# Graph layer kernel: ScalarE copies the edges of all units up to 107 into one PSUM bank, not of the even ones alone

## Chip, cores and metric

One core of a Trainium2 chip. The metric is the device time of one execution in microseconds (us), lower is better.

## What is computed

Two graph layers over 6,250 nodes of 96 features and 106,250 edges sorted by their target node. Cut to what matters (the first layer's call passes `edge_attr_96` as `bases`; `x_feat` is the node table):

```python
h = _gelu(x_feat @ W_pre + b_pre)
msg = h[src] * bases                                  # the product
aggr = jax.ops.segment_sum(msg, dst, num_segments=n)
x = x_feat + aggr
y = _gelu(_gelu(x @ W1 + b1) @ W2 + b2)
return x + y
...
# second layer: the same edges, scaled by 1/sqrt of the degrees
h = x @ W_lin.T + b_lin
agg = jax.ops.segment_sum(h[src] * norm[:, None], dst, num_segments=n)
out = relu(agg + x @ W_root.T + b_root)
# each layer: x = layernorm(x + layer(x))
```

## The kernel before

The edges are cut into tiles of 128, five tiles make a **unit**: 166 units of 640 edges and a tail. What a unit needs:

- **Gather** (GpSimd, L923): five indirect DMAs, one a tile, bring the rows `h[src]` of the unit into the ring `gath`, which has GS = 8 slots. The gather of unit u waits until the product of unit u - 8 is done (`s_msg`). Units 0 to 4 are gathered otherwise, so L923 begins with unit 5.
- **Edges** (SyncE, L741): one DMA brings the edge features into the ring `edg`, ES = 4 slots.
- **One-hots** (VectorE, `hot`, L1352): a matrix per tile that says to which of 64 or 128 target nodes each edge belongs.
- **Product** (VectorE, `multiply`, L1376): `msg` = gathered rows x edges, ring of MS = 5. It reads `gath` in SBUF and, as its other operand, either `edg` in SBUF or the PSUM bank `edges_ps`.
- **Copy** (ScalarE, `copy_edges`, L1086): brings a unit's edges from `edg` into `edges_ps`, one bank for all. `by_bank(u)` (L129) says which units take this way: even ones below AHEAD = 108.
- **Sums** (PE, L1590): five matmuls into `seg` or `seg_odd`, by the parity of the group of units. Groups are three units up to unit 65 and one from unit 66 on, and there even units go to `seg`, odd ones to `seg_odd`. VectorE adds them to `sumT` (L1396).

Beside this, for the second layer, the kernel counts edges between blocks of source nodes and small windows of target nodes. **Pairs** of windows do it: VectorE **builds** the hots of four pairs (L1472 and L1474, two buffers), PE multiplies them (L1622, into `bank_q` and `bank_b` by turns), ScalarE **converts** the counts (`keep_pair`, L1026; where a store ends within a pair, L1029 and L1030). Units 3 to 104 have one or two builds each, so four or eight pairs. The counts go to HBM and come back as **pieces** (`piece_raw`, eight slots) with which PE does the second layer's sums (L1646, 12 matmuls a piece at first) and VectorE adds them (`dense`, L1499). Pieces use `bank_q` and the other bank of that kind; once no more edges are copied, `edges_ps` is their third bank (`last_copied`, `two_banks`). The node steps between the layers (`step0`) run on PE, ScalarE and VectorE in small phases in between.

Nothing is scheduled at run time. `schedule()` makes one list, `order`, and every engine walks it and issues its own part in this order, each waiting on semaphores. For unit u the list has the unit (hot and product on VectorE, sums on PE), the adds, the builds, and then at least eight slots with a pair, a node phase or a piece each. The copy of unit u + 1 stands in slot 2 of unit u:

```python
            if i == 2 and u < UNITS and by_bank(u + 1):
                order.append(("edges", u + 1))
```

So on ScalarE it stands behind the conversions of the first two pairs of unit u and ahead of the others. On PE, `hold` is a small weight load that waits for a semaphore (L1538).

Of the kernel before, what the change touches and what calls it, by code (L numbers as in the profile page):

```python
# [63 lines left out]
AHEAD = 108  # L64
# [63 lines left out]

def by_bank(u):  # L129

    return u % 2 == 0 and u < AHEAD


def reach(g):
# [193 lines left out]
def build(nc, x, xT_in, src, dst, first, tile_first, tile_rows, edge, edge_tail, W_pre, b_pre, W1, b1, W2, b2,  # L328
          WlinT, b_lin, WrootT, b_root, out):
    with ExitStack() as ctx:  # L330
# [3 lines left out]
        def sem(name):  # L334
            return ctx.enter_context(nc.semaphore(name))
# [172 lines left out]
        s_msg = sem("s_msg")  # L508
        s_eps = sem("s_eps")
# [67 lines left out]
        def rooted_before(item):  # L577
# [6 lines left out]
            x[2] == r and order.index(("piece", q)) < last_pair for q, x in enumerate(pieces)))  # L584

        last_copied = max(u for u in range(UNITS) if by_bank(u))
        two_banks = sum(1 for r in range(len(runs)) if any(
            x[2] == r and order.index(("piece", q)) < sums_at(last_copied + 1) for q, x in enumerate(pieces)))
# [64 lines left out]
        def by_tile(bank, tiles, d=D):  # L653
            return bank[:, 0:tiles * d].rearrange("p (t d) -> p t d", d=d)
# [37 lines left out]
        def gathers_before(u):  # L692

            return sum(16 * len(sizes(v)) for v in range(EARLY, u + 1) if v % GS == u % GS)

        def edges_landed(u):
            return sum(16 * (1 if v < UNITS else len(TAILS)) for v in range(u + 1) if v % ES == u % ES)
# [14 lines left out]
        def slot_tiles(u):  # L712

            s = u % GS
            return slice(s * UT, s * UT + len(sizes(u)))
# [269 lines left out]
        def _(act):  # L985
# [92 lines left out]

            def copy_edges(u):
                if u > 0:  # L1080
                    act.wait_ge(s_msg, u - 1)
                else:
                    act.wait_ge(s_kb, 3)
                act.wait_ge(s_edge[u % ES], edges_landed(u))
                if u < UNITS:
                    act.copy(edges_ps[:, 0:UT * D], edg[:, u % ES].rearrange("p j d -> p (j d)")).then_inc(s_eps, 1)  # L1086
                else:
                    for j, k in enumerate(TAILS):
                        last = act.copy(edges_ps[0:k, j * D:(j + 1) * D], edg[0:k, u % ES, j, :])
                    last.then_inc(s_eps, 1)  # L1090

            act.wait_ge(s_w, 8 * 16)
            for item in order:
                what = item[0]
                if what == "edges":
                    copy_edges(item[1])
                elif what == "meta":
                    keep_windows()
                elif what == "pair":
                    keep_pair(item[1])  # L1100
                elif what == "step0":
                    step_0(item[1], item[2], item[2])
                elif what == "step1":
                    step_1(item[1], item[2], item[2])
# [175 lines left out]
        def _(dve):  # L1280
# [82 lines left out]
            def multiply(u):  # L1363
                s = u % MS
                if by_bank(u):
                    dve.wait_ge(s_eps, u // 2 + 1)
                    edges = by_tile(edges_ps, UT)
                else:
                    dve.wait_ge(s_edge[u % ES], edges_landed(u))
                    edges = edg[:, u % ES]  # L1370
                if u < EARLY:
                    dve.wait_ge(s_h, CHUNKS - (-(u + 1) * UT // CT))
                else:
                    dve.wait_ge(s_gath[u % GS], gathers_before(u))
                if u < UNITS:
                    dve.tensor_tensor(  # L1376
                        msg[:, s, :, 0:D], gath[:, slot_tiles(u), :], edges, ALU.mult).then_inc(s_msg, 1)
                else:
                    for j, k in enumerate(TAILS):
                        last = dve.tensor_tensor(msg[0:k, s, j, 0:D], gath[0:k, u % GS * UT + j, :],  # L1380
                                                 edges[0:k, j, :], ALU.mult)
                    last.then_inc(s_msg, 1)
# [118 lines left out]
            for item in order:  # L1501
                what = item[0]
                if what in ("unit", "hot"):
                    hot(item[1])
                if what in ("unit", "product"):
                    multiply(item[1])
                elif what == "add":
                    add(item[1])
                elif what == "meta":
                    merge_windows()  # L1510
                elif what == "flag":
                    judge()
                elif what == "build":
                    build_hots(item[1])
                elif what == "dense":
                    dense(item[1])
                elif what == "step0":
                    node_stage_0(dve, item[1], item[2], item[2])
                elif what == "step1":
                    node_stage_1(dve, item[1], item[2], item[2])  # L1520
# [306 lines left out]
```

## Time and profile before

| | |
|---|---|
| time, median of 3 runs | 1125.99 us (1120.19 to 1127.88) |
| the profiled execution | 1126.56 us |
| its span, first to last instruction | 1124.8 us |
| mean granted TensorE clock in it | 0.906 |
| indirect gathers L923 | 806 |
| products with edges in SBUF / in PSUM | 112 / 54 |

The profile is one execution. A span is the time of one instruction or transfer from start to end; "idle before" is the time for which an engine stood still just before an instruction, with what ended it. "issue" means that the profile shows nothing it waited for. Times in the rows count from the start of the span. PEld is PE's weight load, which overlaps its matmuls. The clock is a share of TensorE's full 2.4 GHz.

### The profile page before, as it was taken

What the parts mean: (1) busy time and instruction counts of PE and PEld (TensorE: products, weight loads), DVE (VectorE), ACT (ScalarE), POOL (GpSimd) and SP (SyncE); (2) the same over time, 40 slices, a digit from 0 to 9 for tenths busy, and PEclk for the clock granted to TensorE, in tenths of its full rate; (3) what the DMA queues carried; (4) which work ended last, traced back from release to release, by engine and by line L of the source; (5) the groups of instructions that cost most, each with busy time, mean ns of one, the idle gap of its engine ahead of it and who ended that gap; (6) DMA issues with size and microseconds to landing.
All of it is one profiled execution on the core that took longest, in us unless ns stands there. A gap on an engine that the chain in (4) does not pass through costs nothing. (4 is left out here: it accounts for less than half of the span.)

```text
span 1124.8 us, 21017 instructions
## 1 busy us (share of the span) xinstructions
PE 938.3 (83%) x7410; PEld 792.9 (70%) x7847; DVE 719.1 (64%) x1521; ACT 473.2 (42%) x884; POOL 833.6 (74%) x917
## 2 busy tenths in 40 slices
PE   5877677677767887898889889899999989889786
PEld 5844445344444775685678678799999989789786
DVE  8976797677767667756576666634336454646567
ACT  1366685665665566555565556600001010001115
POOL 7877777777777777777777777777777777777715
PEclk9997986888877999696699999999999999879898
DMA  9457776675666769777788889998999997767853
GB/s 286 111 156 251 243 227 218 225 231 173 236 212 194 241 217 300 229 239 240 251 259 262 269 292 300 282 286 251 266 269 293 266 257 217 217 167 203 206 127 90
DMA packets 185723, 260.28 MB, mean 231 GB/s; under 512 B 68651, under 2 KB 163883, under 8 KB 179019
## 3 DMA queue, kind: packets, MB, share of 16 engines
q1 hardware_dynamic: 158049, 215.51, 59.7%
q0 software_dynamic: 26992, 42.82, 16.1%
q8 instruction: 61, 1.00, 0.4%
q10 hardware_dynamic: 569, 0.53, 0.2%
q14 instruction: 52, 0.42, 0.1%
HBM read 173.15 MB, written 85.62 MB: 230 GB/s over the span
## 5 line engine op out<-in xcount | busy, mean ns | idle before, releaser
L923 POOL DMA_INDIRECT gath<-table_h,srcs x806 | 784.6, 973 | 245.6 <-issue 242.5
L1646 PE MATMUL bank_q<-piece_raw,early_late 128*96 128x250 bf16 x2805 | 339.1, 273 | 8.2 <-DVE sumT L1499 6.0
L1646 PEld LDWEIGHTS bank_q<-piece_raw,early_late 128*96 128x96 bf16 x2805 | 304.9, 124 | 2.1 <-issue 0.5
L1026 ACT CAST counts_raw<-bank_q 128x490 bf16<-128x490 f32 x300 | 185.2, 617 | 201.9 <-PE bank_q L1622 198.7
L1026 ACT CAST counts_raw<-bank_b 128x490 bf16<-128x490 f32 x300 | 186.2, 621 | 46.8 <-PE bank_b L1622 46.1
L1622 PE MATMUL bank_q<-hots_raw 128*128 128x245 bf16 x626 | 134.9, 300 | 80.2 <-ACT counts_raw L1026 55.1
L1474 DVE TENSOR_TENSOR hots_raw<-counters,kb 128x1960 bf16<-128x1960 bf16 (+1 forms) x157 | 182.5, 1163 | 0.0
L1622 PE MATMUL bank_b<-hots_raw 128*128 128x245 bf16 x624 | 134.9, 301 | 19.9 <-ACT counts_raw L1026 7.1
L1590 PE MATMUL seg<-onehot,msg 128*97 128x64 f32 (+1 forms) x830 | 111.2, 290 | 23.9 <-DVE msg L1376 23.6
L1590 PE MATMUL seg_odd<-onehot,msg 128*97 128x64 f32 (+1 forms) x832 | 108.8, 286 | 23.3 <-DVE msg L1376 22.6
L1590 PEld LDWEIGHTS seg<-onehot,msg 128*97 128x97 f32 x830 | 103.2, 193 | 33.6 <-DVE msg L1376 31.6
L1472 DVE TENSOR_TENSOR hots_raw<-counters,kb 128x1024 bf16<-128x1024 bf16 (+1 forms) x157 | 106.8, 681 | 24.8 <-PE bank_b L1622 24.8
L1590 PEld LDWEIGHTS seg_odd<-onehot,msg 128*97 128x97 f32 x832 | 101.3, 189 | 29.8 <-DVE msg L1376 27.3
L1622 PEld LDWEIGHTS bank_q<-hots_raw 128*128 128x128 bf16 x626 | 44.6, 102 | 110.2 <-ACT counts_raw L1026 99.5
L1038 ACT ACTIVATE y<-bank_a,b1c 96x512 f32<-96x512 f32 (+2 forms) x14 | 8.8, 629 | 236.3 <-PE bank_a L1661 236.2
L1376 DVE TENSOR_TENSOR msg<-gath,edg 128x480 f32<-128x480 f32 x112 | 72.8, 650 | 48.6 <-DMA gath<-table_h,srcs 48.6
L1622 PEld LDWEIGHTS bank_b<-hots_raw 128*128 128x128 bf16 x624 | 50.1, 103 | 75.7 <-ACT counts_raw L1026 68.0
L1352 DVE TENSOR_TENSOR onehot<-counters,rel 128x320 f32<-128x320 f32 (+1 forms) x166 | 102.0, 614 | 0.0
L1376 DVE TENSOR_TENSOR msg<-gath,edges_ps 128x480 f32<-128x480 f32 x54 | 35.2, 652 | 81.1 <-ACT edges_ps L1086 81.0
L1499 DVE TENSOR_TENSOR sumT<-sumT,bank_q 96x250 f32<-96x250 f32 x91 | 37.1, 409 | 70.2 <-PE bank_q L1646 66.3
L1538 PEld LDWEIGHTS <-w_pre 97*128 97x128 bf16 x437 | 45.1, 109 | 51.8 <-DVE hots_raw L1474 27.0
L1646 PE MATMUL edges_ps<-piece_raw,early_late 128*96 128x250 bf16 x648 | 79.5, 273 | 0.0
(237 smaller groups left out, 796.7 us busy)
## 6 DMA issues: line engine op xcount, KB each, us to landing
counts_hbm<-counts_raw SPq DMA_DIRECT2D x50, 1531.2 KB
piece_raw<-counts_hbm SPq DMA_DIRECT2D x250, 250.0 KB
edg<-in_edge SPq DMA_DIRECT2D x166, 240.0 KB
gath<-table_h,srcs POOLq DMA_INDIRECT x806
piece_raw<-counts_hbm SPq DMA_DIRECT2D x38, 125.0 KB
piece_raw<-counts_hbm SPq DMA_DIRECT2D x25, 187.5 KB
counts_raw<-counts_hbm SPq DMA_DIRECT2D x4, 625.0 KB, 6.5
table_h<-stage SPq DMA_DIRECT2D x12, 192.0 KB, 5.4
```

The lines of the kernel that those rows point to most:

```text
L923: pool.indirect_dma_start(gath[0:k, u % GS * UT + j, :], None, table[0], bass.IndirectOffsetOnAxis(ap=srcs[0:k, t:t + 1], axis=0)).then_in ...
L1026: act.copy(counts[:, k % 2, :, i * WD:(i + 2) * WD].rearrange("p a (w n) -> p a w n", w=2), counted).then_inc(s_kept, 1)
L1038: act.activation(y1[0:D, 0:tiles * P], bank_a[0:D, 0:tiles * P], ACT.Gelu, bias=b1c[:, 0:1]).then_inc(s_y1, 1)
L1352: dve.tensor_tensor(onehot[:, s, :, 0:w], iota_ps[:, 0:w].unsqueeze(1).to_broadcast([P, UT, w]), rel[:, u * UT:(u + 1) * UT].unsqueeze(2). ...
L1376: dve.tensor_tensor(msg[:, s, :, 0:D], gath[:, slot_tiles(u), :], edges, ALU.mult).then_inc(s_msg, 1)
L1472: dve.tensor_tensor(hot_b(j)[:, 0:n], iota_b.unsqueeze(1).to_broadcast([P, n, P, 2]), blocks.unsqueeze(2).to_broadcast([P, n, P, 2]), ALU. ...
L1474: dve.tensor_tensor(hot_k(j)[:, 0:n], iota_k.unsqueeze(1).to_broadcast([P, n, KC, 2]), keys.unsqueeze(2).to_broadcast([P, n, KC, 2]), ALU. ...
L1499: dve.tensor_tensor(total, total, run_sum, ALU.add).then_inc(s_dense, 1)
L1538: pe.ldweights(w_pre[:].bitcast(BF16)[:, 0:P])
L1590: last = pe.matmul(group_sum(g), msg[0:k, u % MS, j, :], onehot[0:k, u % MS, j, 0:reach(g)], start=(u == first_unit(g) and j == 0), stop=( ...
L1622: last = pe.matmul(pair_bank(m)[:, w * KC:(w + 1) * KC], hot_b(j)[:, i, :, w], hot_k(j)[:, i, :, w], start=True, stop=True)
L1646: mm = pe.matmul(sums(r)[0:D, 0:DN], parts[:, FINE[c] + i, part, :], rows, start=(first and i == 0 and part == 0), stop=(last and i == til ...
```

## The change

`by_bank` now holds for every unit below 108. The 54 odd units below 108 get a copy, too, and their product reads `edges_ps`. As there is one bank, copy u must wait for product u - 1 (before: for u - 2, the product that had the bank last), and a product counts the copies by units.

```diff
 def by_bank(u):
 
-    return u % 2 == 0 and u < AHEAD
+    return u < AHEAD
...
             def copy_edges(u):
                 if u > 0:
-                    act.wait_ge(s_msg, u - 1)
+                    act.wait_ge(s_msg, u)
                 else:
                     act.wait_ge(s_kb, 3)
...
             def multiply(u):
                 s = u % MS
                 if by_bank(u):
-                    dve.wait_ge(s_eps, u // 2 + 1)
+                    dve.wait_ge(s_eps, u + 1)
                     edges = by_tile(edges_ps, UT)
```

ScalarE's queue of the kernel before, from the conversions of unit 77 over those of unit 78 to the copy of unit 80 (`s_edge0`: the slot of the ring `edg`):

```order
L1026 CAST counts_raw<-bank_b 128x49x10 [waits s_pair]
L1026 CAST counts_raw<-bank_q 128x49x10 [waits s_pair]
L1026 CAST counts_raw<-bank_b 128x49x10 [waits s_pair]
L1026 CAST counts_raw<-bank_q 128x49x10 [waits s_pair]
L1026 CAST counts_raw<-bank_b 128x49x10 [waits s_pair]
L1026 CAST counts_raw<-bank_q 128x49x10 [waits s_pair]
L1026 CAST counts_raw<-bank_b 128x49x10 [waits s_pair]
L1086 COPY edges_ps<-edg 128x480 [waits s_edge0,s_msg]
L1026 CAST counts_raw<-bank_q 128x49x10 [waits s_pair]
```

The same place of ScalarE's queue in the changed kernel:

```order
L1026 CAST counts_raw<-bank_b 128x49x10 [waits s_pair]
L1026 CAST counts_raw<-bank_q 128x49x10 [waits s_pair]
L1026 CAST counts_raw<-bank_b 128x49x10 [waits s_pair]
L1086 COPY edges_ps<-edg 128x480 [waits s_edge3,s_msg]
L1026 CAST counts_raw<-bank_q 128x49x10 [waits s_pair]
L1026 CAST counts_raw<-bank_b 128x49x10 [waits s_pair]
L1026 CAST counts_raw<-bank_q 128x49x10 [waits s_pair]
L1026 CAST counts_raw<-bank_b 128x49x10 [waits s_pair]
L1086 COPY edges_ps<-edg 128x480 [waits s_edge0,s_msg]
L1026 CAST counts_raw<-bank_q 128x49x10 [waits s_pair]
```

A copy for unit 79 has come in behind the first two conversions of unit 78, with the other conversions behind it. The rest of the queue is as it was.

VectorE's queue at unit 79, as a piece of the difference (the product of unit 79, ahead of it the add of a group's sum and the unit's one-hot, behind it the first build of the unit):

```order
 L1396 TENSOR_TENSOR sumT<-sumT,seg_odd 97x64
 L1352 TENSOR_TENSOR onehot<-counters,rel 128x5x64 [waits s_seg]
-L1376 TENSOR_TENSOR msg<-gath,edg 128x5x96 [waits s_gath7,s_edge3]
+L1376 TENSOR_TENSOR msg<-gath,edges_ps 128x5x96 [waits s_gath7,s_eps]
 L1472 TENSOR_TENSOR hots_raw<-counters,kb 128x1024 [waits s_pair]
 L1474 TENSOR_TENSOR hots_raw<-counters,kb 128x1960
```

Nothing changes its place. The product waits for ScalarE's copy (`s_eps`) in place of the edges' transfer (`s_edge3`). The queues of SyncE and GpSimd are the same in both kernels. PE has the same matmuls; from the first run of pieces in `edges_ps` on, the three banks of the runs come in another turn.

## Rows read from the trace of the kernel before

**Rows 1.** Groups by form: count | busy us, mean ns | idle before, what ended it.
```profile
L923 POOL DMA_INDIRECT gath<-table_h,srcs x806 | 784.6, 973 | 245.6 <-issue 242.5 <-DVE msg L1376 3.1
...
L1376 DVE TENSOR_TENSOR msg<-gath,edg 128x480 f32<-128x480 f32 x112 | 72.8, 650 | 48.6 <-DMA gath<-table_h,srcs 48.6
...
L1376 DVE TENSOR_TENSOR msg<-gath,edges_ps 128x480 f32<-128x480 f32 x54 | 35.2, 652 | 81.1 <-ACT edges_ps L1086 81.0
L1086 ACT COPY edges_ps<-edg 128x480 f32<-128x480 f32 x54 | 31.9, 591 | 0.7 <-DVE msg L1376 0.7
```
**Rows 2.** Windows: PE, PEld, DVE, ACT, POOL busy us; clock, DMA, GB/s.
```profile
170.00:383.00 213.00, 151.24 (x861) 99.44 (x923) 152.78 (x243) 129.70 (x242) 161.97 (x168) 0.82 0.66 213
383.00:735.00 352.00, 305.17 (x2422) 254.37 (x2540) 227.81 (x432) 205.16 (x369) 267.57 (x278) 0.91 0.83 261
735.00:968.00 233.00, 229.64 (x2147) 224.72 (x2238) 106.00 (x292) 13.89 (x21) 177.80 (x182) 0.99 0.91 266
968.00:1047.00 79.00, 66.69 (x538) 62.04 (x571) 42.27 (x128) 8.66 (x14) 60.10 (x63) 0.84 0.70 184
```
**Rows 3.** Timeline, gathers and products: start us, us, engine.
```profile
61.25 1.41 POOL L923 DMA_INDIRECT gath<-table_h,srcs  x1 [0.30 <-issue]
...
150.87 0.65 DVE L1376 TENSOR_TENSOR msg<-gath,edg 128x480 f32<-128x480 f32 x1
150.91 1.43 POOL L923 DMA_INDIRECT gath<-table_h,srcs  x1 [0.30 <-issue]
...
158.78 0.65 DVE L1376 TENSOR_TENSOR msg<-gath,edges_ps 128x480 f32<-128x480 f32 x1
158.90 0.94 POOL L923 DMA_INDIRECT gath<-table_h,srcs  x1 [0.30 <-issue]
...
161.39 0.94 POOL L923 DMA_INDIRECT gath<-table_h,srcs  x1 [0.31 <-issue]
161.76 0.65 DVE L1376 TENSOR_TENSOR msg<-gath,edg 128x480 f32<-128x480 f32 x1
...
740.39 1.40 POOL L923 DMA_INDIRECT gath<-table_h,srcs  x1 [0.31 <-issue]
```
**Rows 4.** The line L1376 in 170 to 383 us: what its engine waited for.
```profile
  DMA gath<-table_h,srcs: 32.4, 9
```
**Rows 5.** The same in 383 to 735 us; and who waited for it.
```profile
  ACT edges_ps L1086: 40.1, 18
...
  PEld seg L1590: 6.0, 7
...
  PEld seg_odd L1590: 2.1, 2
```
**Rows 6.** Timeline around unit 79.
```profile
538.66 0.65 DVE L1376 TENSOR_TENSOR msg<-gath,edg 128x480 f32<-128x480 f32 x1
...
539.82 1.17 DVE L1474 TENSOR_TENSOR hots_raw<-counters,kb 128x1960 bf16<-128x1960 bf16 x1
...
543.30 0.61 ACT L1026 CAST counts_raw<-bank_b 128x490 bf16<-128x490 f32 x1
...
545.93 0.62 PE L1622 MATMUL bank_q<-hots_raw 128*128 128x245 bf16 x2
```
**Rows 7.** L923 up to 726.6 us (min/median/max ns, first and last start); timeline there.
```profile
L923 POOL DMA_INDIRECT gath<-table_h,srcs x535: 940/944/1922, 44.8 to 725.4; - x179
...
722.60 0.66 DVE L1376 TENSOR_TENSOR msg<-gath,edges_ps 128x480 f32<-128x480 f32 x1 [0.94 <-ACT edges_ps L1086]
...
726.65 0.94 POOL L923 DMA_INDIRECT gath<-table_h,srcs  x1 [0.30 <-DVE msg L1376]
```
**Rows 8.** The line L1376 in 968 to 1047 us: what its engine waited for.
```profile
  DMA gath<-table_h,srcs: 16.2, 8
```
**Rows 9.** Windows of two stretches of 383 to 735 us.
```profile
441.00:568.00 127.00, 110.58 (x746) 85.80 (x783) 78.35 (x146) 69.72 (x127) 96.55 (x100) 0.77 0.76 240
568.00:735.00 167.00, 146.80 (x1305) 129.78 (x1363) 107.25 (x212) 98.28 (x175) 127.08 (x132) 1.00 0.89 277
```

## Prediction

> **What bounds the kernel now.** I read the groups first, for the engine whose work reaches from end to end. It is GpSimd with its 806 gathers [rows 1]: 784.6 us busy and 242.5 us idle "until issue". These add to 1027 us, and the idle time is the fixed 0.30 us that stands before every gather in the timeline [rows 3]. So GpSimd issues gathers from 44.8 us to about 1074 us with no pause, almost the whole span of 1124.8 us. A gather's median is 944 ns [rows 7] and its mean 973, which leaves 806 x 0.029 = 23 us of stretched gathers.
>
> Next I read the windows by stage [rows 2] and the product's waits [rows 4, 5]. They show who paces whom.
> - 170 to 383 us (units 23 to 56): VectorE waits 32.4 us for gathers before nine products, so the gathers pace.
> - 383 to 735 us (units 57 to 106): no product waits for a gather. PE is busy 305.2 of 352 us, and the products wait only for ScalarE's copies (40.1 us, 18 times). VectorE falls behind the gathers.
> - 735 to 968 us: PE is busy 229.6 of 233 us. What is late at 735 is late at 968.
> - 968 to 1047 us: products wait for gathers again (16.2 us, 8 times) [rows 8]; then comes the end.
>
> How far VectorE falls behind is in [rows 7]: 535 gathers have begun before 726.6, five a unit from unit 5 on, so the one at 726.65 is unit 112's first. It reuses the slot of unit 104, whose product ends at 722.60 + 0.66 = 723.26. GpSimd is 3.4 us from having to wait.
>
> **Removed: VectorE's second SBUF operand in 54 odd products.** A product takes 650 ns from SBUF and 652 ns from PSUM [rows 1], so VectorE itself gains nothing. GpSimd does. In [rows 3] an SBUF product starts at 150.87, the gather at 150.91 takes 1.43 us, 0.49 over the median; at 161.76 one starts inside a running gather, which stays at 0.94; at 158.78 a PSUM product is running when a gather starts, 0.94 again. So only a gather that starts while an SBUF product runs is stretched, to about the product's end. I laid all odd products up to unit 107 beside the gathers: 27 gathers over 1.00 us overlap one, from 61.25 (1.41) to 740.39 (1.40), the first and last in [rows 3], together 9.0 us over the median. 4.1 us lie before 383 us, 4.9 after. In one of them another SBUF operation shares the blame.
>
> The Trainium skill (GPSIMD Engine Reference, Key points) says that GpSimd shares its SBUF interfaces with VectorE, with contention for VectorE instructions with two SBUF inputs. Priced on every product's full length that would be 54 x 0.65 = 35 us, an estimate; the trace narrows it to gathers that begin under a product, 9 us, and the trace decides.
>
> **Added: 54 copies on ScalarE.** 54 x 0.591 = 31.9 us [rows 1]. ScalarE is busy 129.7 of 213 and 205.2 of 352 us in the two middle stages [rows 2], so as plain work they fit. Each stands behind the first two conversions of the unit ahead, and the later conversions stand behind it, so PE gets its bank back up to 0.6 us later.
>
> **The semaphore on the product before.** It adds nothing where hots are built (units 3 to 104): the two conversions ahead of copy u+1 need hots that VectorE builds after product u, so the queue imposes this order already. In units 1 and 3, by hand, the copy would end within 0.02 us of where the product starts now.
>
> **Moved: odd products wait for ScalarE.** This is the real cost. Behind a waiting product on VectorE stand the builds of the hots, and PE's pair products wait for these. Unit 79 [rows 6]: its product runs at 538.66 now, its first build ends at 540.99, 2.33 us after the product's start. The second conversion ahead of copy 79 (the one at 543.30) ends at 543.91; then copy 0.59, product at 544.53, build ready at 546.86. PE begins unit 79's first pair at 545.93, behind the unit's sums: that pair comes 0.9 us later. So a hold of 5.9 us costs PE 0.9, the rest lies under PE's own queue. Done for each of the 24 odd units from 57 to 103, eight holds are between 3.6 and 5.9 us, the others under 2.2 or none. I price six units like unit 79 (5.6 us; in the others PE arrives later than the hots) and 1.4 us for the added copies between conversions: 7 us of new PE waiting in this stage.
>
> The bounds are far apart. From below, even units already run this way: PE's weight loads wait 6.0 us for even products (seg) and 2.1 for odd ones (seg_odd) [rows 5]; doubling the difference adds 3.9 us. From above, all of VectorE's 40.1 us wait happens again and reaches PE: 40 us. I take 7, near the lower row, because that stage's PE idle time, 47 us, is mostly not caused by products.
>
> In 170 to 383 us the same holds come to 18 us (six odd units from 23 to 51), against 32.4 us of waiting for gathers. The gathers keep the pace with 14 us to spare, so this stage takes GpSimd's gain: -4.1 us at unit 57, at worst +4.
>
> **Other edits.** The first use of the copy bank by a piece moves from after unit 106 to after 107 and the banks of later runs rotate; the same matmuls remain. Nothing.
>
> **The sum.** At 735 us products stand at -4.1 + 7 = +2.9 us. GpSimd would be 8.5 us ahead by unit 112 (9.0 less the last stretch), but has only 3.4 us of room: the slot of unit 104 comes free at 723.3 + 2.9 = 726.2, so GpSimd now really waits, about 8 us, and leaves at -0.5 us. From there PE runs full to 968 (+2.9), the gathers run at -0.5. In 968 to 1047 PE idles 12 us and products wait 16.2 us for gathers: a PE chain late by 2.9 us catches up there, down to the gathers' -0.5. The end lies between -0.5 and +2.9; I take +1. The profiled execution took 1126.56 us, its span 1124.8; it lies 0.6 us above the median of 1125.99. 1126.56 + 1 = 1127.6, or 1127.0 beside the median. I say 1127.5. Here 9 us taken from the longest chain buy nothing, since they are used up by a ring of 8 units that has no room.
>
> **Rivals.**
> - **The ScalarE loop paces every unit (slower).** Place: products of odd units in 170 to 735 us. For: 40.1 us of such waits exist in even units alone [rows 5]. It decides once the gathers no longer pace by unit 57: then -4.1 becomes up to +4, and node steps on VectorE, which it now does ahead, show in odd units too; 0.9 us in 16 of the 24 units is 14 us. +4 + 14 = +18, less 2 absorbed behind 968: 1143. Against: 124 us of VectorE's 352 are idle. Chance 0.2.
> - **The clock (slower).** PE's granted clock is 0.77 in 441 to 568 us, where it is busy 110.6 of 127, and 1.00 in 568 to 735, busy 146.8 of 167 [rows 9]. 0.77 is a mean over stretches at 1.2 and at 2.4 GHz. If new gaps bring 0.77 to the second stretch, it can deliver 129 of its 146.8 us of busy work: 18 us at most, half of it 9: 1136. The Trainium skill (TensorE: Matmul & The Clock Gate, Part 1) ties this clock to PE's recent activity; by it new gaps could cost a stretch at 1.2 GHz, and no row here shows how many it would be. Chance 0.12.
> - **The gain arrives whole.** If a queue of ScalarE that is ahead hides the holds, and the PE-bound stage starts 9 us earlier: 1126.56 - 9.0 = 1117.6. Against: 3.4 us of room, and 12 us of PE idle behind 968. Chance 0.12.
> - The forecast, 1121 to 1134, has 0.5; 0.06 is for what I have not seen.
>
> **Range and chances.** 1118 to 1143 leaves out less than 2 in 10. What a measurement of this kernel tells from no change is about 1%, 11.3 us. Faster by more than that needs more than the 9.0 us there is: 0.04. Slower by more (from 1137.3) is the first slower rival and a third of the second: 0.22. Within: 0.74.
>
> **What would show it.** Right: edges_ps products x108, of which over 35 wait for L1086, some 80 us in 383 to 735; gathers at a median of 944 ns with total busy near 776 us; GpSimd waiting some 8 us for products between 640 and 740 us, where it waits for none now; PE idle up by 7 in 383 to 735; lag gone by 980. Wrong: products of 170 to 383 that never wait for gathers (first rival), a clock below 1.00 in 568 to 735 (second), no GpSimd wait at all and 735 reached 5 us earlier (third).

## The result and the profile after

The changed kernel takes 1135.0 us, the median of nine runs (1130.4 to 1137.99), beside 1122.65 us for the kernel before in as many (1120.19 to 1127.88). The ratio is 1.0094, with a 95% interval of 1.0077 to 1.0111: slower by just under 1%, 12.35 us between the medians. I had forecast 1127.5 us, no change that can be told. That stood on a median of three runs, 1125.99 us; against either median my forecast is a change of some +1 us, and 12.35 us came. One run of those told below, of `r_h` at 2104.54 us, stands in no median and no ratio. The profiled execution took 1135.81 us with a span of 1134.0 us (before: 1126.56 and 1124.8), at a mean granted clock of 0.901 (0.906).

The groups by form of the changed kernel, beside [rows 1]:

```profile
L923 POOL DMA_INDIRECT gath<-table_h,srcs x806 | 779.5, 967 | 263.4 <-issue 238.5 <-DVE msg L1376 24.9
...
L1376 DVE TENSOR_TENSOR msg<-gath,edges_ps 128x480 f32<-128x480 f32 x108 | 70.3, 651 | 169.1 <-ACT edges_ps L1086 168.8
L1086 ACT COPY edges_ps<-edg 128x480 f32<-128x480 f32 x108 | 63.4, 587 | 7.7 <-DVE msg L1376 7.7
L1376 DVE TENSOR_TENSOR msg<-gath,edg 128x480 f32<-128x480 f32 x58 | 37.7, 650 | 12.9 <-DMA gath<-table_h,srcs 12.9
```

The first row holds most of the case. The gathers' own time fell from 784.6 to 779.5 us, as it was meant to, by 5.1 us. Their idle time rose from 245.6 to 263.4 us, by 17.8 us, because GpSimd now waits 24.9 us for products where it had waited 3.1. The balance is +12.7 us, and the last gather starts at 1086.45 us, 12.6 us later than before. These two executions differ by 9.25 us in time, since from the start of the last gather to the end of the span the one before took 50.9 us and this one 47.6. The profiled execution of before is 3.9 us over its median; that 12.6 lies so near the 12.35 us of the medians is chance. The second row is why: products wait 168.8 us for copies in place of 81.0.

The windows, beside [rows 2] and [rows 9]:

```profile
170.00:383.00 213.00, 158.83 (x866) 103.64 (x928) 157.09 (x254) 141.41 (x268) 161.37 (x170) 0.81 0.65 213
383.00:735.00 352.00, 301.47 (x2358) 249.62 (x2477) 225.51 (x422) 211.57 (x387) 253.78 (x267) 0.91 0.80 255
735.00:968.00 233.00, 227.73 (x2124) 221.73 (x2210) 105.24 (x291) 20.86 (x33) 177.59 (x180) 0.99 0.89 263
968.00:1047.00 79.00, 70.83 (x564) 66.44 (x598) 43.74 (x131) 8.67 (x14) 60.41 (x62) 0.83 0.69 193
...
441.00:568.00 127.00, 108.47 (x733) 83.14 (x771) 78.68 (x144) 72.10 (x134) 96.23 (x102) 0.78 0.77 244
568.00:735.00 167.00, 145.68 (x1254) 128.01 (x1313) 104.76 (x205) 99.74 (x181) 113.74 (x120) 0.98 0.83 264
```

In 383 to 735 us GpSimd is busy 253.8 us instead of 267.6, PE 301.5 instead of 305.2: both lost time there. The clock in 568 to 735 us is 0.98, where it was 1.00: the sign that I had written down for the clock rival. It is small, but it will count below.

The product's waits, first in 170 to 383 us, beside [rows 4]:

```profile
  ACT edges_ps L1086: 52.8, 20
```

and in 383 to 735 us, beside [rows 5]:

```profile
  ACT edges_ps L1086: 83.5, 37
...
  POOL gath L923: 20.3, 11
  PEld seg L1590: 7.1, 8
  PEld seg_odd L1590: 6.0, 7
```

In the first of the two, "DMA gath" is gone from the list: where nine products had waited 32.4 us for gathers, none does now. In the second, the line "POOL gath" stands among those that wait for the product: GpSimd, 11 times, 20.3 us. PE's waits for odd products (seg_odd) rose from 2.1 to 6.0 us, by the 3.9 us of my lower bound.

How far each stage moved is read from the start of one product in both timelines (unit 56 ends the first stage, 104 the PE-bound one) and from the gathers. I give the changed kernel twice: the first execution, and one of a second measurement that is told below (`after_again`).

| start, us against before | changed | changed, again |
|---|---|---|
| first gather of unit 56 | -4.0 | -5.4 |
| product 56 (383.0) | +3.4 | -1.5 |
| product 96 | +6.4 | +1.6 |
| product 104 (722.6) | +11.7 | +6.8 |
| first gather of unit 112 (726.6) | +9.0 | +4.1 |
| product 147 (970.8) | +11.3 | +6.4 |
| last gather (1073.9) | +12.6 | +7.2 |
| time of these executions (1126.56) | +9.3 | +3.8 |
| time, medians | +12.4 | +6.9 |

### The profile page after: what moved, and what is told of

The parts are those of the page before. It is cut to its first block and busy times, and to the rows that moved or that the text cites. A ratio compares the mean times of both kernels' runs of the same rounds, so it can differ in the third digit from the quotient of the medians.

```text
span 1134.0 us, 21125 instructions
## 1 busy us (share of the span) xinstructions
PE 945.3 (83%) x7410; PEld 796.3 (70%) x7847; DVE 719.5 (63%) x1521; ACT 496.7 (44%) x938; POOL 828.6 (73%) x917
## 5 line engine op out<-in xcount | busy, mean ns | idle before, releaser
L923 POOL DMA_INDIRECT gath<-table_h,srcs x806 | 779.5, 967 | 263.4 <-issue 238.5
L1474 DVE TENSOR_TENSOR hots_raw<-counters,kb 128x1960 bf16<-128x1960 bf16 (+1 forms) x157 | 182.4, 1162 | 0.0
L1376 DVE TENSOR_TENSOR msg<-gath,edges_ps 128x480 f32<-128x480 f32 x108 | 70.3, 651 | 169.1 <-ACT edges_ps L1086 168.8
L1590 PE MATMUL seg<-onehot,msg 128*97 128x64 f32 (+1 forms) x830 | 114.9, 296 | 19.4 <-DVE msg L1376 19.2
L1590 PEld LDWEIGHTS seg<-onehot,msg 128*97 128x97 f32 x830 | 106.0, 197 | 30.1 <-DVE msg L1376 28.1
L1646 PEld LDWEIGHTS edges_ps<-piece_raw,early_late 128*96 128x96 bf16 x666 | 70.3, 123 | 0.0
```

What stands on the lines that cost most here:

```text
L923: pool.indirect_dma_start(gath[0:k, u % GS * UT + j, :], None, table[0], bass.IndirectOffsetOnAxis(ap=srcs[0:k, t:t + 1], axis=0)).then_in ...
L1376: dve.tensor_tensor(msg[:, s, :, 0:D], gath[:, slot_tiles(u), :], edges, ALU.mult).then_inc(s_msg, 1)
L1474: dve.tensor_tensor(hot_k(j)[:, 0:n], iota_k.unsqueeze(1).to_broadcast([P, n, KC, 2]), keys.unsqueeze(2).to_broadcast([P, n, KC, 2]), ALU. ...
L1590: last = pe.matmul(group_sum(g), msg[0:k, u % MS, j, :], onehot[0:k, u % MS, j, 0:reach(g)], start=(u == first_unit(g) and j == 0), stop=( ...
L1646: mm = pe.matmul(sums(r)[0:D, 0:DN], parts[:, FINE[c] + i, part, :], rows, start=(first and i == 0 and part == 0), stop=(last and i == til ...
```

## The experiments

All stand beside runs of the kernel before on the same chip, and a ratio is that of the kernel to it. They came in four sets. The diffs are against the changed kernel unless another is named.

**First set: what the parts do alone.** The change has three parts: relief (odd products don't read a second operand from SBUF), the work of 54 copies, and the hold (an odd product waits for ScalarE's queue).

`r_only` is the relief alone: the kernel before, in which odd products read the bank as it stands (the diff is against the kernel before; the pieces' first use of the bank is also moved behind unit 107, as in the change).

```diff
-                if by_bank(u):
+                if u < AHEAD:
                     dve.wait_ge(s_eps, u // 2 + 1)
+                    dve.wait_ge(s_edge[u % ES], edges_landed(u))
                     edges = by_tile(edges_ps, UT)
```

> Odd products up to unit 107 read the PSUM bank as it stands (the edges of the unit before, so the sums of odd units are left wrong), without a copy and without a wait for one. This is the relief of GpSimd alone. Theory 'hold' (odd products that wait for ScalarE are the loss): nothing is held, so this is faster than before by what the gather-paced stage can use, about 4 us: ratio 0.996; the product of unit 56 about 4 us earlier than before, that of unit 165 about 4 earlier. Rival 'all of it carries': 9 us, 0.992. Rival 'the PSUM operand itself costs': slower than before.

Measured: 1118.29 us, ratio 0.9968 [0.9953, 0.9983]. So the relief is worth 0.32% here, about 3.6 us (by the interval 1.9 to 5.3) of the 9 that I had counted. Its row of gathers shows where the gain comes from:

```profile
L923 POOL DMA_INDIRECT gath<-table_h,srcs x806 | 777.0, 964 | 245.8 <-issue 242.5 <-DVE msg L1377 3.3
```

The gathers are 7.6 us shorter in all, and GpSimd waits no more than before.

`c_only` is the copies' work alone: odd copies take a constant and odd products don't wait for them.

```diff
+                if u > 0:
+                    act.wait_ge(s_eps, u)
+                if u % 2 == 1:
+                    act.copy(by_tile(edges_ps, UT), iota[:, 0:D].unsqueeze(1).to_broadcast([P, UT, D])
+                             ).then_inc(s_eps, 1)
+                    return
...
-                if by_bank(u):
+                if by_bank(u) and u % 2 == 0:
```

> ScalarE makes the 54 added copies at their places (of a constant of the same shape, into the same bank), but odd products read SBUF and wait for nothing, as before. This is the copies' work alone. Theory 'hold': within 2 us of before, ratio 1.000 to 1.002. Rival 'work' (the copies push conversions and so PE's banks): 54 x about 0.2 us or more, 1.008 and up; the product of unit 56 late by 5 us or more against before.

Measured: 1124.18 us, ratio 1.0007 [0.9993, 1.0022]. 31.6 us of copies (54 of 0.585 us) are hidden as work, and what they do to PE's banks is too small to be told here.

`h_only` is the hold alone, with a copy of one column (0.194 us) in the place of the full one; odd products wait for it and read `edg`.

```diff
+                if u % 2 == 1:
+                    act.copy(tiny[:, 0:1], iota[:, 0:1]).then_inc(s_eps, 1)
+                    return
...
-                else:
+                if not by_bank(u) or u % 2 == 1:
                     dve.wait_ge(s_edge[u % ES], edges_landed(u))
                     edges = edg[:, u % ES]
```

> Odd products wait for ScalarE at the same place of its queue as in the change, but what stands there is a copy of one column, and they read SBUF as before. This is the hold alone. Theory 'hold': slower than before by all of the change's loss and the relief that it lacks, 12 to 16 us, ratio 1.011 to 1.014, with the product of unit 56 late by 5 or more. Rival 'work': nearly as before, under 4 us, 1.003.

Measured: 1127.28 us, ratio 1.0036 [1.0021, 1.0050]. These are 4 us where the theory of the hold wanted 12 to 16: the hold behind a short copy is not the whole loss.

`r_h` is both: the same small copy, and odd products read the bank as it stands.

```diff
+                if u % 2 == 1:
+                    act.copy(tiny[:, 0:1], iota[:, 0:1]).then_inc(s_eps, 1)
+                    return
...
                     dve.wait_ge(s_eps, u + 1)
+                    dve.wait_ge(s_edge[u % ES], edges_landed(u))
```

> The hold with a copy of one column, and odd products read the bank as it stands (sums of odd units left wrong): relief and hold, without the copies' work. Theory 'hold': as the change less up to 3 us, ratio 1.007 to 1.010. Rival 'work': 0.996 to 0.999.

Measured: 1121.64 us, ratio 0.9996 [0.9980, 1.0012], where 1.007 to 1.010 was expected. Relief and hold cancel, and the relief is worth 0.40% under this short hold. But the three parts add up to 1.0011 (0.9968, 1.0007 and 1.0036), and the whole is 1.0094. Something in the whole is more than its parts: the full copy in front of a held product had been in none of these kernels.

**Second set: the copy's length under the hold, and its place.** `full_front` keeps everything of the change but the relief: odd products wait for the full copy and read `edg`.

```diff
                 if by_bank(u):
                     dve.wait_ge(s_eps, u + 1)
                     edges = by_tile(edges_ps, UT)
-                else:
+                if not by_bank(u) or u % 2 == 1:
                     dve.wait_ge(s_edge[u % ES], edges_landed(u))
                     edges = edg[:, u % ES]
```

> The change, but odd products read SBUF again: they still wait for the full copy of their edges, whose result they do not use. Theory 'length' (a held product pays for the length of the copy in front of it, 0.59 in place of 0.19 us, since conversions, copy, product, hots and pairs close a loop): the change without its relief, 1.0094 + 0.003 = 1.012 to 1.013, about 9 us over the hold with the short copy. Rival 'work and hold add up': 1.0036 + 0.0007 = 1.004.

Measured: 1133.34 us, ratio 1.0089 [1.0067, 1.0111]. That is far above the rival's 1.004, and under the 1.012 to 1.013 that came from adding the relief to the first 1.0094.

`full_behind` has the small copy release the product and the full one stand right behind it, so ScalarE does the same work and more. Odd products read `edg`, by the same edit as in `full_front`.

```diff
+                if u % 2 == 1:
+                    act.copy(tiny[:, 0:1], iota[:, 0:1]).then_inc(s_eps, 1)
+                    act.copy(by_tile(edges_ps, UT), iota[:, 0:D].unsqueeze(1).to_broadcast([P, UT, D])
+                             ).then_inc(s_behind, 1)
+                    return
+                if u > 0:
+                    act.wait_ge(s_behind, u // 2)
```

> Odd products read SBUF and wait for a copy of one column; a full copy of a constant follows right behind it on ScalarE. The same work and hold as in the run before, but the length stands behind what releases the product. Theory 'length in front': 1.0036 + 0.0007 = about 1.004. Rival 'length behind' (the later conversions, and so PE's banks, are what a held loop pays for): 1.010 and up, like the run before.

Measured: 1125.98 us, ratio 1.0017 [1.0000, 1.0035]. The two differ by 0.72% and the intervals don't touch. Odd products read SBUF in both. What moved is whether 0.59 us of copy end before the product or after it. (The later one copies a constant and doesn't wait for the edges' transfer, but `full_front` shows no copy that waited for a transfer either.) The group rows of the two kernels, first `full_front`:

```profile
L923 POOL DMA_INDIRECT gath<-table_h,srcs x806 | 782.6, 971 | 256.7 <-issue 241.0 <-DVE msg L1376 15.8
```

and `full_behind`:

```profile
L925 POOL DMA_INDIRECT gath<-table_h,srcs x806 | 781.2, 969 | 248.9 <-issue 241.9 <-DVE msg L1385 7.0
```

With the copy in front GpSimd waits 15.8 us for products, with it behind 7.0.

Where the difference arises says more. From product 56 to 104 the two take 349.0 and 345.1 us, and 3.0 of these 3.9 us lie between products 96 and 104. The windows from product 96 to 104 of the kernel before, the changed one, `full_front` and `full_behind`, in this order:

```profile
669.54:722.60 53.06, 48.12 (x440) 43.67 (x458) 35.29 (x73) 33.84 (x60) 40.56 (x42) 1.00 0.91 291
675.95:734.26 58.31, 50.94 (x440) 44.99 (x458) 35.30 (x73) 35.66 (x64) 36.82 (x39) 0.97 0.85 266
672.80:731.08 58.28, 50.91 (x440) 45.08 (x458) 35.32 (x74) 35.66 (x64) 36.86 (x39) 0.97 0.85 266
669.37:724.67 55.30, 48.95 (x440) 43.67 (x458) 35.33 (x73) 35.85 (x68) 39.76 (x42) 1.00 0.90 283
```

The same 440 matmuls keep PE busy 2.0 us longer in `full_front`, at a granted clock of 0.97 instead of 1.00, and it idles 1.0 us more. So the length in front costs here partly by waiting and, for the larger part of these 3.0 us, by a stretch at the lower clock that the kernel with the shorter hold does not get.

`all_slot0` is the changed kernel with the copy of unit u + 1 ahead of all of unit u's conversions, `even_slot0` the kernel before with the same edit.

```diff
-            if i == 2 and u < UNITS and by_bank(u + 1):
+            if i == 0 and u < UNITS and by_bank(u + 1):
                 order.append(("edges", u + 1))
```

> The change with the copies two slots earlier: copy u+1 ahead of the conversions of unit u, behind the product of unit u. Theory 'loop': the two conversions leave the way to the next product, so hardly any product waits for ScalarE; the relief stays: 0.994 to 0.997 of before. Rival 'ScalarE blocked' (it now stands still for product u, since the semaphore on the product before binds, with conversions behind it): 1.000 to 1.005.

> The kernel before with its 54 copies two slots earlier. Theory 'loop': the 81 us for which even products wait for ScalarE go, but the gathers pace up to unit 56 and from 148 on: 0.997 to 1.000. Rival: no effect, 1.000 to 1.001.

Measured: `all_slot0` 1116.62 us (1115.75 to 1118.75), ratio 0.9935 [0.9914, 0.9956]; `even_slot0` 1122.17 us, ratio 0.9982 [0.9968, 0.9996]. The same 108 copies that cost 0.6 to 0.9% in slot 2 gain 0.65% in slot 0. The groups of `all_slot0`:

```profile
L923 POOL DMA_INDIRECT gath<-table_h,srcs x806 | 778.6, 966 | 245.6 <-issue 243.4 <-DVE msg L1376 2.1
...
L1376 DVE TENSOR_TENSOR msg<-gath,edges_ps 128x480 f32<-128x480 f32 x108 | 69.9, 647 | 96.4 <-DMA gath<-table_h,srcs 61.5 <-ACT edges_ps L1086 34.7
L1086 ACT COPY edges_ps<-edg 128x480 f32<-128x480 f32 x108 | 62.3, 577 | 28.1 <-DVE msg L1376 28.1
```

Beside the changed kernel, the products' wait for copies fell from 168.8 to 34.7 us and GpSimd's wait for products from 24.9 to 2.1. Now the copies wait for products instead (28.1 us), and products wait for gathers (61.5 us): the gathers pace again in more places, and there their relief is worth something. `even_slot0` is the check on it. Its product 104 starts 11.8 us earlier than before, yet its last gather is only 0.4 us earlier, and its time 0.18% less: what PE's stage gained there ran into the gathers.

**Third set: where, and how long.** `odd_below57` copies the edges of odd units only below 57, `odd_from57` only from 57 on. The waits' counts follow.

```diff
-    return u < AHEAD
+    return u < AHEAD and (u % 2 == 0 or u < 57)
...
-                    act.wait_ge(s_msg, u)
+                    act.wait_ge(s_msg, max(v for v in range(u) if by_bank(v)) + 1)
...
-                    dve.wait_ge(s_eps, u + 1)
+                    dve.wait_ge(s_eps, sum(1 for v in range(u + 1) if by_bank(v)))
```

> The change for odd units below 57 alone; odd units from 57 on read SBUF as before. If the change's loss is the sum of its stages (+3.4 us at the product of unit 56, +8.3 between those of 56 and 104, in the two profiles): +3.4 at unit 56 and about as much at the end, ratio 1.001 to 1.004. Rival 'only the PE-bound stage loses': 1.000 or below.

> The change for odd units from 57 on alone. By the sum of the stages: 0 at unit 56, +8.3 at unit 104, +6 to +8 at the end, ratio 1.005 to 1.007, together with the run before about the change's 1.0094. Rival 'a late start into the stage is what makes it lose': under 1.003.

Measured: `odd_below57` 1121.61 us, ratio 0.9968 [0.9953, 0.9982]; `odd_from57` 1132.23 us, ratio 1.0071 [1.0057, 1.0086]. The first is below the 1.001 to 1.004 that came from the first profile's +3.4 us at product 56; its rival came, that only the PE-bound stage loses. The same change gains 0.3% in its first half and costs 0.7% in its second.

`two_tiles` lets the odd copies bring two of the five tiles (192 of 480 columns, 0.344 us).

```diff
-                if u < UNITS:
+                if u % 2 == 1:
+                    act.copy(edges_ps[:, 0:2 * D], edg[:, u % ES, 0:2].rearrange("p j d -> p (j d)")).then_inc(s_eps, 1)
+                elif u < UNITS:
```

> The change with odd copies of two of the five tiles (192 of 480 columns; the rest of the bank stays stale, so the sums of odd units are left wrong). Theory 'length': about 0.35 us per copy lies 0.16 over the short copy's 0.19 of 0.40 to the full one, so 40% of the way from 0.9996 to 1.0094: 1.002 to 1.005. Rival 'a threshold' (nothing until the loop is longer than the gathers' pace of 6.25 us a unit): 1.000 to 1.001, or the full 1.009.

Measured: 1125.85 us, ratio 1.0013 [1.0000, 1.0027]. By product starts, units 56 to 104 take 345.9 us here, between the 344.4 of `h_only` (copy 0.194 us) and the 347.9 of the changed kernel (0.587 us); before 339.6. So, by one execution each, nearly 5 us of the loss come with the queue place and some 3.5 with the copy's length; of the 3.5, 3.0 lie between products 96 and 104, as above.

**Fourth set: is it repeatable, and is there a middle?** `after_again`, `below57_again` and `from57_again` are the changed kernel and the two halves once more, on one chip, and `all_slot1` has the copy behind one conversion (`i == 1`).

> The changed kernel once more, on one chip with its two halves below. Theory 'the stages add': ratio (0.997 + 1.007 - 1) = 1.004, and a product of unit 56 at about 380 us in this profile (it was 386.4 in the first, 382.0 and 380.4 in two kernels with the same start). Rival 'interaction': 1.009 again, with a product of unit 56 near 386.

> The change below unit 57 alone, once more. 'The stages add' and 'interaction' both say 0.997. If the start varies from execution to execution, the product of unit 56 lies anywhere from 380 to 386 us.

> The change from unit 57 on alone, once more: 1.006 to 1.008, product of unit 56 at 383 us, of unit 104 at 731 to 733.

> The change with the copies one slot earlier: behind one conversion of the unit ahead instead of two. Theory 'loop length': between the change (1.0094) and copies ahead of both (0.9935): 0.996 to 1.004. Rival 'only the semaphore-bound place helps': 1.007 or more.

Measured: the changed kernel 1130.16 us (1127.52 to 1132.6), ratio 1.0056 [1.0034, 1.0079]; first half 0.9975 [0.9964, 0.9987]; second half 1.0083 [1.0063, 1.0104]; `all_slot1` 1117.67 us, ratio 0.9948 [0.9929, 0.9967], a little better than the 0.996 to 1.004 expected. One conversion less in front of the copy turns 1.0056 into 0.9948.

The halves were reproduced, and add up to 1.0058 on this chip, which is the whole there. The whole itself was not reproduced: 1.0056 lies below the first interval, and the two intervals only touch. The slower result, the sign and the mechanism stand in both.

**What all of them have in common.** The start of product 104 and of the last gather against the kernel before, the time of the same execution against the profiled 1126.56 us of before, and the median against that of before in the same set, in us:

| kernel | product 104 | last gather | time of that execution | time, medians |
|---|---|---|---|---|
| changed, first | +11.7 | +12.6 | +9.3 | +12.4 |
| odd_from57, again | +8.0 | +8.7 | +5.8 | +10.3 |
| full_front | +8.5 | +7.9 | +5.1 | +9.4 |
| odd_from57 | +9.4 | +8.5 | +5.6 | +8.3 |
| changed, again | +6.8 | +7.2 | +3.8 | +6.9 |
| h_only | +5.4 | +4.3 | +2.0 | +3.8 |
| two_tiles | +5.3 | +5.6 | +4.1 | +1.9 |
| full_behind | +2.1 | -0.2 | -1.5 | +2.1 |
| c_only | -2.7 | -0.5 | -2.5 | +0.7 |
| r_h | -1.3 | -3.3 | -5.0 | -1.8 |
| odd_below57 | -2.3 | -2.9 | -4.2 | -2.3 |
| odd_below57, again | -1.0 | -2.1 | -4.6 | -2.7 |
| even_slot0 | -11.8 | -0.4 | -1.6 | -1.7 |
| r_only | -7.0 | -8.6 | -12.1 | -5.2 |
| all_slot1 | -8.6 | -7.7 | -9.7 | -5.6 |
| all_slot0 | -16.0 | -7.3 | -7.8 | -7.3 |

The time follows the last gather. The median does so within 4 us in all rows and within 2 in twelve of the sixteen; the time of the same execution lies below it in all sixteen, by 0.5 to 3.5 us and 2.2 in the mean, so the end behind the last gather was somewhat long in the one execution of before. It does not follow product 104: `even_slot0` and `all_slot0` show that. Where products are late, they drag the gathers along; where they are early, the gathers need not come with them. (`two_tiles` was profiled in the slowest of its twelve runs, 1130.68 us, and `r_only` in its fastest, 1114.44, which is part of why their medians fit least.)

## Why the prediction was wrong

The frame held: GpSimd's gathers are the longest chain, their relief was to be given back at the ring of eight slots, and the hold costs PE time in 383 to 735 us. The sum came out too low by its inputs: +1 us, where +12.35 and then +6.9 were measured. Step by step:

- **The relief, -9.0 us.** `r_only` has gathers shorter by 7.6 us, and over the whole it is worth 3.6 us. The Trainium skill (GPSIMD Engine Reference, Key points) speaks of contention with VectorE instructions with two SBUF inputs. The runs agree: with the second operand in PSUM the gathers' mean falls from 973 to 964 ns and the kernel gets faster. My reading of a stretched gather was loose: it does not end with the product, as the one at 150.91 in [rows 3] ends at 152.34, 0.82 us behind the product's end. In the 24 of my 27 that start while the product runs, the time over 0.944 us is what was left of the product less 0.12 us, within 0.01. The other three (units 15, 71, 73) start ahead of the product and under another VectorE instruction that reads SBUF, not one as I had noted. In the changed kernel only 5.1 us of the gathers' time goes. From unit 112 on, where nothing was changed, their stretches came to 13.0 us against 10.2 before (summed over 0.944 us): products that still read SBUF fell otherwise against them.
- **The step that failed first in the run of the program: "The gathers keep the pace with 14 us to spare, so this stage takes GpSimd's gain: -4.1 us at unit 57."** The gathers were 4.0 us earlier at unit 56, as forecast. The products were not: +3.4 us in the one execution, -1.5 in the other. They no longer waited for gathers at all, the sign that I had written down for the first rival. I had compared the sum of the holds (18 us) with the sum of the waits for gathers (32.4 us) and left out what the products bring with them into the stage. These are the last products before it and at its start, units 19, 21 and 23 of the changed kernel:

```profile
156.98 0.65 DVE L1376 TENSOR_TENSOR msg<-gath,edges_ps 128x480 f32<-128x480 f32 x1 [4.77 <-ACT edges_ps L1086]
...
169.76 0.66 DVE L1376 TENSOR_TENSOR msg<-gath,edges_ps 128x480 f32<-128x480 f32 x1 [2.15 <-ACT edges_ps L1086]
...
181.39 0.65 DVE L1376 TENSOR_TENSOR msg<-gath,edges_ps 128x480 f32<-128x480 f32 x1 [2.93 <-ACT edges_ps L1086]
```

- From product 18 to product 23 it now takes 32.3 us (149.1 to 181.4) in place of 22.5, and product 23 starts 11.0 us late. My count of holds began at unit 23. The products then win some of that back, but they walk behind the gathers at ScalarE's pace, held 52.8 us by copies. Still, the term is not far off in time: `odd_below57`, this stage's share alone, gained 0.32 and 0.25%, 3.6 and 2.8 us, beside my 4.1. With it alone, products of unit 56 are 2.6 and 1.2 us early (and within 0.4 us of before in the two executions of `odd_from57`, where nothing is changed up to there). What failed is that the products would take all of it, with certainty.
- **The hold in 383 to 735 us, +7.** From product 56 to 104 it takes 347.9 us in both executions of the changed kernel instead of 339.6: +8.3. With `odd_from57` it is +9.6 and +8.3. The mechanism at unit 79, beside [rows 6]:

```profile
546.36 0.61 ACT L1026 CAST counts_raw<-bank_b 128x490 bf16<-128x490 f32 x1
...
546.85 0.59 ACT L1086 COPY edges_ps<-edg 128x480 f32<-128x480 f32 x1
...
547.47 0.65 DVE L1376 TENSOR_TENSOR msg<-gath,edges_ps 128x480 f32<-128x480 f32 x1 [5.68 <-ACT edges_ps L1086]
...
548.65 1.17 DVE L1474 TENSOR_TENSOR hots_raw<-counters,kb 128x1960 bf16<-128x1960 bf16 x1
...
549.92 0.59 PE L1622 MATMUL bank_q<-hots_raw 128*128 128x245 bf16 x2
```

- Conversion, copy, product, builds, pair: each begins at about the end of the one above it (a first build of 0.68 us lies between the product and the L1474 shown). Product 78 starts 3.06 us later than before, and the pair at 549.92 instead of 545.93 is 3.99 later, so unit 79 adds 0.93 us, where I had said 0.9. But the loss isn't spread as I had priced it, and that my 7 came near 8.3 is partly luck. From product 56 to 96 only 3.0 us are lost, none of them behind 88, and then 5.3 us come between 96 and 104. There the odd products 97, 99 and 103 are held long; these are 99 and 103:

```profile
698.61 0.65 DVE L1376 TENSOR_TENSOR msg<-gath,edges_ps 128x480 f32<-128x480 f32 x1 [4.95 <-ACT edges_ps L1086]
...
728.46 0.65 DVE L1376 TENSOR_TENSOR msg<-gath,edges_ps 128x480 f32<-128x480 f32 x1 [3.44 <-ACT edges_ps L1086]
```

- Of these 5.3 us PE is busy 2.8 and idle the other 2.4 (the windows from product 96 to 104 above). Just behind the hold of product 99, from 701.1 to 704.5 us, its clock stands at 0.5; in the 3.4 us before that it was busy 2.18 us at 0.99. The kernel before has 1.00 in this whole stretch, and so has `full_behind`.
- That the copy's 0.59 us belong to this price, on the path and not "between conversions", is shown by `full_front` against `full_behind`: 0.72%. A part that only delays ScalarE (`c_only`) costs nothing that can be told.
- **"GpSimd now really waits, about 8 us, and leaves at -0.5."** The rule was right, its input was not. By unit 96 the gathers were 6.7 us early (again: 9.2), and with product 104 at +11.7 (+6.8) less the room they stood at +9.0 (+4.1) at unit 112: 2.7 us of the 3.4 us of room were used. So GpSimd's lateness is the product's less 2.7 us, and 20.3 us of waiting instead of 8. The first rows of the timeline that answer to [rows 7] are product 104 and unit 112's first gather of the second execution, then the same gather of the first:

```profile
729.40 0.66 DVE L1376 TENSOR_TENSOR msg<-gath,edges_ps 128x480 f32<-128x480 f32 x1 [0.93 <-ACT edges_ps L1086]
...
730.77 0.94 POOL L923 DMA_INDIRECT gath<-table_h,srcs  x1 [0.30 <-issue]
```

```profile
735.62 0.95 POOL L923 DMA_INDIRECT gath<-table_h,srcs  x1 [0.30 <-issue]
```

- **"A PE chain late by 2.9 us catches up there, down to the gathers' -0.5."** The place exists: from product 147 to the last one, 9.7 us are left of 11.3. But the end follows the gathers, and these were late themselves. They lost a further 3.6 us (again: 3.1) behind unit 112, by the stretches told above and some 0.8 us of waits. So the 3.4 us of room that was to keep part of the relief kept nothing at the end. With -1.5 + 8.3 = +6.8 at product 104 the end came at +6.9 in the second measurement, with 3.4 + 8.3 = +11.7 at +12.4 in the first. I had +2.9 there and took +1.
- **The miss by terms.** In the second measurement 5.9 us lie between my +1 and the +6.9: 2.6 from the first stage (-1.5 for -4.1), 1.3 from the hold (+8.3 for +7), 2.0 from the catching up that did not come. In the first the same terms are 7.5, 1.3 and 2.6 us of 11.4. (Product starts are of one execution each and the end is a median.)
- **The first rival** had the place and the sign right and its size too high: 1143 rests on 0.9 us in 16 of 24 units, 14 us, beside 8.3 measured. **The clock rival** had place and sign right as well and is part of the loss: the clock in 568 to 735 us fell from 1.00 to 0.98, by two stretches of 3.4 us at 0.5 (from 595.2 and from 701.1 us), where I had allowed for 9 to 18 us. (The kernel before has one such stretch, from 496.0 us, that the changed one has not, so from product 56 to 104 it is one more.) Against `full_behind` the second is worth the 2.0 us of PE time told above. **The gain whole** needed a queue ahead of the products, and `all_slot0` shows that it is to be had by moving the copy: 1116.62 us beside the 1117.6 that I gave that case.

**What stays open.** Why the changed kernel measured 1.0094 first and 1.0056 later. In the profiled executions the difference arises before unit 56 (product 56 at 386.4 and at 381.5 us), and the granted clock in 170 to 383 us was 0.81 in the first and 0.86 in the second, whose window is

```profile
170.00:383.00 213.00, 155.91 (x911) 103.20 (x974) 160.98 (x258) 144.46 (x275) 160.98 (x170) 0.86 0.67 216
```

Over half of it can be seen between products 36 and 40, here in the first execution of the changed kernel, in the second, and in the repetition of `odd_below57`, which has the same instructions there:

```profile
260.38:286.50 26.12, 20.47 (x101) 14.76 (x106) 19.30 (x31) 15.58 (x31) 19.73 (x22) 0.73 0.53 166
261.92:285.25 23.33, 17.52 (x101) 12.03 (x106) 19.23 (x31) 15.57 (x31) 17.55 (x19) 0.84 0.60 186
259.27:281.55 22.28, 16.08 (x101) 10.54 (x106) 19.29 (x31) 15.56 (x31) 16.80 (x19) 0.92 0.62 192
```

The same 101 matmuls keep PE busy 20.47, 17.52 and 16.08 us at a granted clock of 0.73, 0.84 and 0.92, and the stretch is longer by nearly that much; VectorE and ScalarE are busy as long in all three.

Kernels with the same instructions up to there (`odd_below57`, its repetition, `full_front` in all but one operand) have product 56 between 380.4 and 382.0 us. So the late product 56 of the first execution goes with a lower clock. Why the clock was lower there, and whether this is what separates the two medians, stays open: no run set it apart, and it is one execution against several. The value of the relief under the full hold is open by as much: `full_front` at 1.0089 stands beside 1.0094 (worth nothing) or 1.0056 (worth 0.3%).

## What to carry to other kernels

The price of a wait on an engine with a fixed queue is decided by what stands ahead of the awaited instruction there: the same 54 copies cost 0.6 to 0.9% behind two conversions and gain 0.5 to 0.65% behind one or none. Work added to an engine that has time costs only if someone waits for its end; then its length counts too, though not evenly: three quarters of what it cost here in units 56 to 104 fell in the last eight of them, with a stretch at the lower clock. So compare PE's busy time for the same matmuls before a longer stage is put down to waiting alone. Before relief of the pace-setting engine is booked as a gain, walk its margin through the program from the start, unit by unit, and follow the ring that ties it to its consumer: a sum of waits over a stage says nothing on who leads at its entry.

## What the runs showed beyond the expected

- A stage can be freed by far more than the program gains. In `even_slot0` units 56 to 104 take 326.0 us instead of 339.6, 13.6 us less, and the time falls by under 2 us; only with the gathers relieved as well (`all_slot0`, 329.1 us) does it fall by 7.3. Most of the 13.6 us is not idle time saved but PE's own: it is busy 10.3 us less, at a clock of 0.94 instead of 0.91, with 2323 matmuls in place of 2329. The window from product 56 to 104 before, and in `even_slot0`:

```profile
383.03:722.60 339.57, 294.66 (x2329) 245.00 (x2443) 221.19 (x417) 198.98 (x359) 258.18 (x268) 0.91 0.83 262
384.79:710.83 326.04, 284.32 (x2323) 238.56 (x2438) 220.62 (x419) 198.71 (x359) 247.77 (x257) 0.94 0.86 270
```

- The relief saved between 5 and 7.6 us of the gathers' time, not the 9 counted, and the stretches that remain in the unchanged part differ with how products fall against gathers: 10.2 us of them from unit 112 on before, 13.0 in the changed kernel, with the same instructions.
- A third of the full copy's time is there with a single column: 0.194 us for one column, 0.344 for 192, 0.587 for 480, so about 0.8 ns for each further column.
